# Self attention without its handover stalls, and the channel norm in three steps: one edit of a twelve-stage kernel

## The chip, the cores and the metric

The kernel runs on one core of a Trainium2 chip. The metric is the device time of one execution in microseconds (us). The engines are named as in the profile: PE is TensorE's matmuls, PEld its weight loads, DVE VectorE, ACT ScalarE, POOL GpSimd, SP the engine whose queue starts the transfers.

## The reference, cut to what matters

A tensor x of 16 blocks (batch) x 128 tokens x 256 channels passes through twelve sublayers, each `x = layernorm(x + sublayer(x))`. Three of them carry the change:

```python
# stage 1, self attention inside each block of 128 tokens
q, k, v = x @ Wq + bq, x @ Wk + bk, x @ Wv + bv
x = layernorm(x + softmax(q @ k.T / 16 + mask) @ v)
# stages 7 and 10, attention over channels (8 heads of 32 channels; the tokens are in pairs of halves)
ret = softmax(q.T @ k * scale) @ v.T           # q from x, k and v from a context of the same size
x = layernorm(x + ret)                         # stage 10 multiplies ret by gamma
# stage 11, int8-like feed forward; its weights are scaled by their largest magnitude
s = max(abs(W)); Wq = clip(round(W * 127 / s), -127, 127)
```

Stage 0, the gated delta rule, comes before stage 1 and only its end is touched.

## The kernel before, in words

The program is written engine by engine: each stage is a class with one method for each engine, and a stage's `order()` yields the steps that every engine walks in the same order. An engine executes its instructions strictly in that order and waits on counting semaphores (`wait_ge`). So a step that waits holds up all that is behind it on that engine. Tokens are worked on in 4 groups of 4 blocks (512 tokens). `X` holds x by tokens, `xT` its transposed copy. A sublayer ends for a group with a norm on DVE (4 `bn_stats` L211, 4 `bn_aggr` L214, a reciprocal root of 12 dependent operations on 4 numbers a partition L190 to L203, 4 scalings L227, which count `xn` up) and a "turn": 8 transposes on PE (L172), two copies on ACT (L181), which count `xt` up. `room[b]` is what must have happened before PSUM bank b may be written again.

**Delta rule, stage 0.** For the last group the steps are "close" (sum, L776), "stats", "scale" and "turn". At its end every bank is set to wait for the last turn: `for b in range(8): room[b] = c.xt.at(16)`.

**Self attention, stage 1.** The order is, for t = 0 to 4: "qk" (group t; 4 times 2 matmuls L285, 4 drains on ACT L896), "pt" (t - 1; 4 transposes L871, a copy L907), "v" (t; L291, 2 drains on DVE L920), "o" (t - 1; L880), "s" (t; scores L863, then on DVE scale and mask L924 and row maxima L927, then 4 exponentials on ACT L902), "close" (t - 1). "close" is on DVE the sum into the one tile R (L934) and the whole norm, and on PE and ACT the turn of the same group. ACT, DVE and SP enter the stage when the whole turn of stage 0 is done (`before`, `may_load`); PE waits for `dma[0] >= 64`, that is for all four transfers: weights, two biases and the mask, whose 1 MB comes in pieces of 512 bytes.

**Channel attention, stages 7 and 10** (Channels, ChannelsGamma). For t = 0 to 18 a step t works on block t and the two before it. PE runs "sh" (2 transposes of the negated maxima of block t - 1, L2498), "s" 0 (scores of block t, L2489), "t" 0 (transposed scores of block t - 1, L2510), "o" 0, "t" 1, "s" 1, "o" 1, "t" 2, "vt" (context of block t + 1 turned, L2478), "o" 2, "t" 3 (L2523 is "o"). DVE takes 4 maxima after each "s" (L2585, about 0.62 us each from start to start), shifts (L2591, "sh") and finishes block t - 3 (L2597 to L2605, "mul"). "t" 0 on PE waits for "sh" on DVE. POOL masks the operands of the next block (L2629, L2632) and v (L2638) when ACT has copied what "vt" turned. The norm of a group is "stats" (L211 to L203, all but the scalings) and "scale" (L227), at t = 6 and 7, 10 and 11, 14 and 15, and after the loop. Both stand between "t" 1 and "s" 1. The turn of the group is at t = 8, 12, 16 and at the end, after "vt", in bank 7 alone; stage 10 leaves its turns out.

**Beside stage 10** the steps of `Quant.BESIDE` prepare stage 11, one per t, behind "s" 1: "wmax" (the largest of each partition), "wall" (largest over the partitions: a transpose L2234, a maximum on DVE L2337, a broadcasting matmul L2236, four small DVE operations L2339 to L2342, all in bank 7), "wround" (ACT L2286, then POOL clips L2397), "wcast", and "xmax", "xround", "xclip", "xcast" for the first tokens. Within "wall" PE waits for DVE's maximum before it goes on to the matmul.

Of the kernel before, what the change touches and what calls it, by code (L numbers as in the profile page):

```python
# [65 lines left out]
class Core:  # L66
# [139 lines left out]
    def moments(self, dve, own, rows, st, sw, eps):  # L206

        for j, (row, ready) in enumerate(rows):
            if ready:
                dve.wait_ge(own.sem, ready)  # L210
            o = own(dve.bn_stats(st[:, j, 0:6], row))  # L211
        dve.wait_ge(own.sem, o)
        for j in range(4):
            o = own(dve.bn_aggr(st[:, j, 6:8], st[:, j, 0:6]))  # L214
        dve.wait_ge(own.sem, o)
        return self.rsqrt(dve, own, st[:, :, 7:8].rearrange("p a b -> p (a b)"), eps, [sw[:, blk(i, 4)] for i in range(3)])
# [78 lines left out]
class Delta(Stage):  # L295
# [131 lines left out]
    def order(self):  # L427


        for t in range(self.U + self.LAG + 5):  # L430
# [4 lines left out]
            for step, u in every:  # L435
                if 0 <= u < self.U and (step not in ("close", "stats", "scale", "turn") or u % 16 == 15):
                    yield step, u, u % self.RING, u // 16, u % 16

    def tensor(self, pe):
# [122 lines left out]
        for b in range(8):  # L562
            room[b] = c.xt.at(16)
# [248 lines left out]
class SelfAttention(Stage):  # L812


    def weights(self):
        c = self.c
        self.w, self.b, self.bv = c.f32("aw", 3, 2, D), c.f32("ab", 4), c.f32("abv", D)
        self.mask = c.f32("amask", NB, T)

    def load(self, sp):  # L820
        i = self.ins
        self.may_load(sp)
        self.fetch(sp, 0, (self.w[:, :, :, :], i["a_w"].rearrange("n (c p) f -> p n c f", p=128)), (self.b[:, :], i["a_b"]),
                   (self.bv[:, :], i["a_bv"]), (self.mask[:, :, :], i["mask_BxSxS2_ff0"].rearrange("b q k -> q b k")))

    def buffers(self):
        c = self.c
        self.QK, self.V = c.sets(2, "aQK", 2, 2, 512), c.sets(2, "aV", 4, D)
# [4 lines left out]
        self.vc, self.sm, self.mx = v("v", 8), v("s", 4), v("max", 4)  # L833

    def order(self):
        for t in range(5):
            for step, u in (("qk", t), ("pt", t - 1), ("v", t), ("o", t - 1), ("s", t), ("close", t - 1)):
                if 0 <= u < 4:
                    yield step, u, u % 2

    def tensor(self, pe):
        c, bank, room = self.c, self.c.bank, self.c.room
        pe.wait_ge(self.dma[0], 64)
        for step, g, s in self.order():
# [29 lines left out]
            elif step == "o":  # L874
                pe.wait_ge(*self.ptc.at(g + 1))
                pe.wait_ge(*self.vc.at(2 * g + 2))
                for b in range(4):
# [3 lines left out]
                    room[b // 2] = c.xn.at(4 * self.n + g + 1)  # L881
                t.then_inc(*self.o.up)
            elif step == "close":
                c.turn_tensor(pe, self.n, g, (2, 3))

    def scalar(self, act, own):
        c, bank = self.c, self.c.bank
        self.before(act)
        act.wait_ge(self.dma[0], 64)
        for step, g, s in self.order():  # L890
# [17 lines left out]
            elif step == "close":  # L908
                c.turn_scalar(act, self.n, g, (2, 3))

    def vector(self, dve, own):
        c, bank = self.c, self.c.bank
        self.before(dve)
        dve.wait_ge(self.dma[0], 64)
        for step, g, s in self.order():
# [6 lines left out]
            elif step == "s":  # L922
                dve.wait_ge(*self.sc.at(g + 1))
                dve.scalar_tensor_tensor(out=self.S[s][:, :, :], in0=g4(bank(6)), scalar=1.0 / 16, in1=self.mask[:, blk(g, 4), :],  # L924
# [6 lines left out]
            elif step == "close":  # L931
# [2468 lines left out]
```

## Time and profile before

| | |
|---|---|
| median of 3 runs | 4642.03 us (4641.69 to 4643.85) |
| profiled execution, its own time | 4642.03 us |
| its span, first to last instruction | 4640.2 us |
| mean granted TensorE clock | 0.901 of full |
| self attention with the norm and turn before it | 1178.4 to 1304.0 us of the span |
| channel attention, stages 7 and 10 | 2736.7 to 2976 us and 4274 to 4521 us |

The span is 1.8 us shorter than the execution's own time. A busy time is that of an engine's instructions; where an engine is idle the profile names the instruction of another engine whose signal ended the idle time.

### The profile page before, as it was taken

The page shows a single profiled execution, that of the slowest core. Times are in us where ns is not written, and L with a number is a line of the kernel's source. Part 1 is how long each engine was busy: PE and PEld are TensorE (multiplying, and loading weights), DVE is VectorE, ACT ScalarE, POOL GpSimd, SP SyncE. Part 2 cuts the span into 40 slices and gives each one's busy share as a digit, 9 for nine tenths or more (in the row PEclk, how much of TensorE's full clock was granted, in tenths as well). Part 3 has the DMA queues.
Part 4 walks back from the last instruction along what each step waited for, and adds up shares of the span by engine and source line. Part 5 has one row for each costly group of instructions (what it writes and reads, how often), then busy time and mean ns, then how long its engine had stood idle before and what let it go on. Part 6 is the DMA issues. An engine that isn't in the chain of part 4 may idle for free. (4 is left out here: it accounts for less than half of the span.)

```text
span 4640.2 us, 69825 instructions
## 1 busy us (share of the span) xinstructions
PE 3831.6 (83%) x25178; PEld 2327.9 (50%) x25196; DVE 3215.6 (69%) x7121; ACT 1966.2 (42%) x4633; POOL 1140.9 (25%) x1338
## 2 busy tenths in 40 slices
PE   7799999999615757778888889676999999897985
PEld 3466666656413435545455555453555555454543
DVE  7789989886376764432455557656888888886678
ACT  4466666655201013311333324324655556564345
POOL 2423333233021225220111122003332323233220
PEclk9899999999757878879899989888999999998797
DMA  2322222221101000020000000200000000001000
GB/s 63 75 61 65 62 65 63 56 56 42 39 31 31 1 0 21 1 67 0 20 1 1 1 28 2 113 1 0 1 1 1 1 1 1 1 1 44 1 1 19
DMA packets 220694, 120.64 MB, mean 26 GB/s; under 512 B 114881, under 2 KB 213057, under 8 KB 219137
## 3 DMA queue, kind: packets, MB, share of 16 engines
q1 hardware_dynamic: 220352, 116.17, 9.0%
q8 instruction: 204, 3.34, 0.3%
q14 instruction: 138, 1.12, 0.1%
HBM read 101.42 MB, written 14.68 MB: 25 GB/s over the span
## 5 line engine op out<-in xcount | busy, mean ns | idle before, releaser
L285 PE MATMUL ps<-xT,min 128*128 128x512 f32 (+1 forms) x1072 | 539.4, 633 | 7.7 <-DVE mZ L3121 5.4
L3126 DVE SCALAR_TENSOR_TENSOR macc<-ps,mcw,macc 128x508 f32<-128x508 f32 (+2 forms) x408 | 302.9, 743 | 149.7 <-ACT macc L3048 140.1
L3062 ACT ACTIVATE mE<-ps,mcol 128x128 f32<-128x128 f32 x1024 | 291.3, 370 | 8.1 <-PE ps L2960 1.0
L3212 POOL TENSOR_TENSOR mE<-mE,mCB 128x512 f32<-128x512 f32 x128 | 163.7, 1279 | 498.3 <-ACT mE L3062 498.3
L285 PEld LDWEIGHTS ps<-xT,min 128*128 128x128 f32 (+1 forms) x1072 | 184.9, 193 | 192.9 <-issue 182.6
L172 PE MATMUL ps<-ident,X 128*128 128x128 f32 x352 | 77.7, 388 | 239.9 <-DVE X L227 206.7
L2990 PE MATMUL ps<-mwo,macc 128*128 128x256 f32 x1024 | 245.4, 383 | 15.6 <-DVE macc L3160 15.6
L2553 ACT ACTIVATE hE<-ps 128x512 f32<-128x512 f32 x256 | 139.0, 595 | 248.9 <-PE ps L2510 248.9
L3219 POOL TENSOR_TENSOR mSQ<-mSQ,mtn 128x512 f32<-128x512 f32 x128 | 163.4, 1277 | 257.8 <-ACT mtn L3066 257.8
L2175 POOL TENSOR_TENSOR lP<-lP,lm 128x512 f32<-128x512 f32 x64 | 66.6, 1041 | 610.3 <-DVE lm L2157 610.3
L2990 PEld LDWEIGHTS ps<-mwo,macc 128*128 128x128 f32 x1024 | 185.8, 191 | 42.8 <-DVE macc L3160 21.2
L2091 ACT ACTIVATE lP<-ps,lm 128x128 f32<-128x128 f32 x256 | 90.6, 366 | 268.0 <-DVE lm L2153 268.0
L2585 DVE TENSOR_REDUCE hMX<-ps 128x2 f32<-128x512 f32 x256 | 159.0, 685 | 55.8 <-PE ps L2489 55.8
L181 ACT COPY xT<-ps 128x512 f32<-128x512 f32 x88 | 50.6, 587 | 342.5 <-PE ps L172 342.4
L803 POOL TENSOR_TENSOR dTB<-did,dNB 128x1024 f32<-128x1024 f32 (+1 forms) x10 | 29.2, 2919 | 665.9 <-DMA dNB<-d_N 601.3
L172 PEld LDWEIGHTS ps<-ident,X 128*128 128x128 f32 x352 | 60.5, 202 | 255.8 <-DVE X L227 214.8
L808 POOL TENSOR_TENSOR dTB<-dTB,dtmp 128x30 f32<-128x30 f32 (+11 forms) x300 | 170.1, 567 | 23.5
L709 DVE SCALAR_TENSOR_TENSOR dav<-ps,dsmall,dav 128x508 f32<-128x508 f32 (+2 forms) x192 | 142.4, 741 | 47.8 <-ACT dav L580 43.3
L709 DVE SCALAR_TENSOR_TENSOR daq<-ps,dsmall,daq 128x508 f32<-128x508 f32 (+2 forms) x192 | 142.5, 742 | 40.0 <-ACT daq L580 34.4
L2510 PE MATMUL ps<-hXE,hKE 32*128 32x256 f32 x1024 | 162.0, 438 | 8.1 <-ACT hE L2553 5.8
L807 POOL TENSOR_TENSOR dtmp<-dNB,dTB 128x30 f32<-128x30 f32 (+11 forms) x300 | 153.2, 511 | 23.5
L477 PE MATMUL ps<-dKQ 128*128 128x256 f32 x512 | 136.7, 394 | 26.7 <-ACT dO L655 19.0
(582 smaller groups left out, 9559.4 us busy)
## 6 DMA issues: line engine op xcount, KB each, us to landing
dwk<-in_L_attn_Wk SPq DMA_DIRECT2D x64, 128.0 KB, 2.3
dwq<-in_L_attn_Wq SPq DMA_DIRECT2D x64, 128.0 KB, 2.3
dwv<-in_L_attn_Wv SPq DMA_DIRECT2D x64, 128.0 KB, 2.4
dwg<-in_L_attn_Wg SPq DMA_DIRECT2D x64, 128.0 KB, 2.4
dwo<-in_L_attn_Wo SPq DMA_DIRECT2D x64, 128.0 KB, 2.6
min<-in_m_in SPq DMA_DIRECT2D x2, 4096.0 KB, 17.3
d_N<-dNT SPq DMA_DIRECT2D x256, 16.0 KB, 1.5
dTT<-d_TT SPq DMA_DIRECT2D x256, 16.0 KB, 1.9
```

Of the source, the lines that this page charges most:

```text
L285: t = pe.matmul(out, w[:, j, :], self.c.xT[:, j, blk(g, 512)], start=j == 0, stop=j == 1)
L709: x = dve.scalar_tensor_tensor(out=acc[:, :, 3 - j:T], in0=p[:, :, 0:T - 3 + j], scalar=small[:, 4 * k + j:4 * k + j + 1], in1=acc[:, :, 3 ...
L807: then(pool.tensor_tensor(part, bc(NB[:, s, s + 1:32], s, True), bc(TB[:, s, 0:s], 31 - s), ALU.mult))
L808: then(pool.tensor_tensor(low, low, part, ALU.subtract))
L2510: t = pe.matmul(bank(4 + i)[:, blk(lt, 256)], self.KE[x][r, e, blk(lt)], self.XE[x][r, e, :], start=True, stop=True)
L2553: a = act.activation(self.E[y][:, 2 * (2 * rr + i) + e, :, :], bank(4 + i).rearrange("p (n q) -> p n q", n=2), ACT.Exp, scale=0.25)
L2585: m = dve.tensor_reduce(self.MX[y][:, k, 32 * r:32 * r + 32:16], bank(r).rearrange("p (e n) -> p e n", e=2), AX.X, ALU.max, negate=True)
L2990: t = pe.matmul(bank(j // 2)[:, blk(j % 2, 256)], self.acc[s][:, blk(j)], self.wo[:, i, :], start=i == 0 and j % 2 == 0, stop=i == 31 and ...
L3062: x = act.activation(self.E[s][:, e, blk(j)], bank(4 + e)[:, blk(j)], ACT.Exp, bias=self.col[:, 4 * g + j, 0, 2 * i + e:2 * i + e + 1])
L3126: x = dve.scalar_tensor_tensor(out=acc[:, :, 3 - j:T], in0=p[:, :, 0:T - 3 + j], scalar=self.cw[:, i, j:j + 1], in1=acc[:, :, 3 - j:T], op ...
L3212: pool.tensor_tensor(g4(self.E[s][:, 0, :]), g4(self.E[s][:, 0, :]), self.CB[g % 2][:, :, :], ALU.mult).then_inc(*self.m0.up)
L3219: pool.tensor_tensor(self.SQ[g % 2][:, :], self.SQ[g % 2][:, :], self.tn[s][:, :], ALU.add).then_inc(*self.sqa.up)
```

## The change

Self attention: (1) its weights get a place that stage 0 does not use and are fetched without a wait; the mask is fetched apart, on a semaphore of its own, when stage 0's last norm is done, and only DVE's "s" step waits for it. (2) The turn of stage 0's last group moves out of stage 0 and behind the first "qk" and "v" ("last"). (3) "close" falls apart into "sum" (its own semaphore, two tiles R in turn), "norm" one round later, between "pt" and "v", and "turn" at the end of that round. Channel attention: the norm is in three steps, "stats", "rsqrt", "scale", at t = 6, 7, 8 and so on, all behind "s" 1 now; the turns are one t later. Beside stage 10 "wall" is in two steps, "wturn" and "wall", two t apart, and the later steps move.

```diff
@@ Delta
-                if 0 <= u < self.U and (step not in ("close", "stats", "scale", "turn") or u % 16 == 15):
+                if 0 <= u < self.U and (step not in ("close", "stats", "scale", "turn") or u % 16 == 15) and (step, u) != ("turn", self.U - 1):
...
-        for b in range(8):
-            room[b] = c.xt.at(16)
@@ SelfAttention
+    LOADS, PLACE, REST = 2, 154944, 0
...
     def load(self, sp):
         i = self.ins
-        self.may_load(sp)
         self.fetch(sp, 0, (self.w[:, :, :, :], i["a_w"].rearrange("n (c p) f -> p n c f", p=128)), (self.b[:, :], i["a_b"]),
-                   (self.bv[:, :], i["a_bv"]), (self.mask[:, :, :], i["mask_BxSxS2_ff0"].rearrange("b q k -> q b k")))
+                   (self.bv[:, :], i["a_bv"]))
+        sp.wait_ge(*self.c.xn.at(4 * self.n))
+        self.fetch(sp, 1, (self.mask[:, :, :], i["mask_BxSxS2_ff0"].rearrange("b q k -> q b k")))
...
+        self.mask, self.R = c.f32("amask", NB, T), [c.R, c.f32("aR", 4, D)]
...
     def order(self):
-        for t in range(5):
-            for step, u in (("qk", t), ("pt", t - 1), ("v", t), ("o", t - 1), ("s", t), ("close", t - 1)):
-                if 0 <= u < 4:
+
+        for t in range(6):
+            for step, u in (("qk", t), ("pt", t - 1), ("norm", t - 2), ("v", t), ("last", t), ("o", t - 1), ("sum", t - 1), ("s", t), ("turn", t - 2)):
+                if 0 <= u < (1 if step == "last" else 4):
                     yield step, u, u % 2
...
-        pe.wait_ge(self.dma[0], 64)
+        pe.wait_ge(self.dma[0], 48)
...
-                    room[b // 2] = c.xn.at(4 * self.n + g + 1)
+                    room[b // 2] = self.su.at(g + 1)
                 t.then_inc(*self.o.up)
-            elif step == "close":
+            elif step == "last":
+                c.turn_tensor(pe, self.n - 1, 3, (2, 3))
+            elif step == "turn":
                 c.turn_tensor(pe, self.n, g, (2, 3))
...
     def scalar(self, act, own):
         c, bank = self.c, self.c.bank
-        self.before(act)
-        act.wait_ge(self.dma[0], 64)
+        act.wait_ge(*c.xn.at(4 * self.n))
+        act.wait_ge(self.dma[0], 48)
...
     def vector(self, dve, own):
         c, bank = self.c, self.c.bank
-        self.before(dve)
-        dve.wait_ge(self.dma[0], 64)
+        dve.wait_ge(self.dma[0], 48)
...
                 dve.wait_ge(*self.sc.at(g + 1))
+                dve.wait_ge(self.dma[1], 16)
...
-            elif step == "close":
+            elif step == "sum":
                 dve.wait_ge(*self.o.at(g + 1))
                 dve.wait_ge(own.sem, self.r)
-                sums = [own(dve.scalar_tensor_tensor(out=c.R[:, j, :], in0=bank(j // 2)[:, blk(j % 2, 256)], scalar=m[:, 8 + j:9 + j],
-                                                     in1=c.X[:, 4 * g + j, :], op0=ALU.mult, op1=ALU.add)) for j in range(4)]
-                c.norm_vector(dve, own, self.n, g, sums)
+                for j in range(4):
+                    x = dve.scalar_tensor_tensor(out=self.R[s][:, j, :], in0=bank(j // 2)[:, blk(j % 2, 256)], scalar=m[:, 8 + j:9 + j],
+                                                 in1=c.X[:, 4 * g + j, :], op0=ALU.mult, op1=ALU.add)
+                x.then_inc(*self.su.up)
+            elif step == "norm":
+                dve.wait_ge(*self.su.at(g + 1))
+                c.norm_vector(dve, own, self.n, g, [0] * 4, self.R[s])
@@ Quant
-    BESIDE = {3: ("wmax", 0), 4: ("wmax", 1), 5: ("wall", 0), 6: ("wall", 1), 7: ("wround", 0), 8: ("wround", 1), 10: ("wcast", 0), 12: ("wcast", 1),
-              13: ("xmax", 0), 14: ("xround", 0), 15: ("xclip", 0), 16: ("xcast", 0)}
+    BESIDE = {3: ("wmax", 0), 4: ("wmax", 1), 5: ("wturn", 0), 6: ("wturn", 1), 7: ("wall", 0), 8: ("wall", 1), 9: ("wround", 0), 10: ("wround", 1),
+              11: ("wcast", 0), 12: ("wcast", 1), 13: ("xmax", 0), 14: ("xround", 0), 15: ("xclip", 0), 16: ("xcast", 0)}
...
     def tensor_step(self, pe, step, u):
         c, bank, room = self.c, self.c.bank, self.c.room
-        if step == "wall":
+        if step == "wturn":
             pe.wait_ge(*room[7])
             pe.wait_ge(*self.wm.at(u + 1))
             pe.transpose(bank(7)[0:1, 0:128], self.g1[:, u:u + 1], c.ident[:, :]).then_inc(*self.wt.up)
+            room[7] = self.wm.at(u + 3)
+        elif step == "wall":
+            pe.wait_ge(*room[7])
@@ Channels
-                if step == "t" and k == 1:
-                    for n, first in (("stats", 6), ("scale", 7)):
+                if step == "s" and k == 1:
+                    for n, first in (("stats", 6), ("rsqrt", 7), ("scale", 8)):
                         if t >= first and (t - first) % 4 == 0:
                             yield n, (t - first) // 4, 0
-                if step == "s" and k == 1 and t in self.ASIDE:
-                    yield "aside", *self.ASIDE[t]
-                if step == "vt" and t >= 8 and t % 4 == 0 and self.TURNS:
-                    yield "turn", (t - 8) // 4, 0
+                    if t in self.ASIDE:
+                        yield "aside", *self.ASIDE[t]
+                if step == "vt" and t >= 9 and t % 4 == 1 and self.TURNS:
+                    yield "turn", (t - 9) // 4, 0
+        yield "rsqrt", 3, 0
```

`moments` is cut in two helpers, `moments_of` (L211, L214) and `rsqrt_of` (L190 to L203), which issue the same instructions.

## Rows read from the trace of the kernel before

**Rows 1.** The page: busy time of each engine, share of the span, instructions.

```profile
PE 3831.6 (83%) x25178; PEld 2327.9 (50%) x25196; DVE 3215.6 (69%) x7121; ACT 1966.2 (42%) x4633; POOL 1140.9 (25%) x1338
```

**Rows 2.** Stretch of self attention: busy us of each engine (instructions), clock, DMA.

```profile
1178.36:1304.04 125.68, 73.98 (x280) 50.00 (x280) 44.47 (x160) 25.24 (x62) 0.00 (x0) 0.79 0.10 35
```

**Rows 3.** What PE waited for there: us in total, times, longest.

```profile
PE ps L172 <- DVE X L227: 40.2, 5, 8.6
PE ps L285 <- DMA amask<-in_mask_BxSxS_ff: 10.2, 1, 10.2
```

**Rows 4.** Timeline, stage 0's end and the start: start, us, instruction, [idle before].

```profile
1178.36 1.42 DVE L776 TENSOR_TENSOR R<-ps,X 128x256 f32<-128x256 f32 x4 [3.87 <-PE ps L555]
...
1184.05 1.38 DVE L227 TENSOR_SCALAR X<-R,st,rsq 128x256 f32<-128x256 f32 x4
...
1189.77 0.84 SPq L276 DMA_DIRECT2D amask<-in_mask_BxSxS_ff  x1
...
1197.63 9.70 PE L285 MATMUL ps<-xT,aw 128*128 128x512 f32 x16 [10.17 <-DMA amask<-in_mask_BxSxS_ff]
```

**Rows 5.** Timeline, the second round of PE: first qk, pt, and the scores.

```profile
1212.40 7.03 PE L285 MATMUL ps<-xT,aw 128*128 128x512 f32 x16
1219.27 0.60 PE L871 MATMUL ps<-ident,aP 128*128 128x128 f32 x4
...
1224.89 1.95 PE L863 MATMUL ps<-aQK 128*128 128x128 f32 x16
```

**Rows 6.** Timeline: the third sum, PE's stall behind it, the stage's last copy.

```profile
1281.41 1.65 DVE L934 SCALAR_TENSOR_TENSOR R<-ps,am,X 128x256 f32<-128x256 f32 x4
...
1288.64 1.97 PE L172 MATMUL ps<-ident,X 128*128 128x128 f32 x8 [8.60 <-DVE X L227]
...
1303.42 0.59 ACT L181 COPY xT<-ps 128x512 f32<-128x512 f32 x1 [0.27 <-PE ps L172]
```

**Rows 7.** Stage 7: one plain step t; then t = 6 and 7; 10 and 11; 14 and 15.

```profile
2798.32:2809.08 10.76, 10.76 (x136) 6.45 (x137) 8.27 (x14) 5.20 (x11) 3.41 (x7) 1.00 0.01 3
2809.08:2837.84 28.76, 24.72 (x268) 14.70 (x269) 23.09 (x51) 10.39 (x21) 6.83 (x13) 0.88 0.00 1
2863.80:2892.48 28.68, 24.67 (x268) 14.41 (x268) 23.08 (x50) 10.39 (x21) 6.82 (x13) 0.88 0.01 2
2918.44:2946.57 28.13, 24.31 (x262) 13.94 (x262) 22.58 (x50) 10.06 (x20) 3.54 (x7) 0.88 0.01 1
```

**Rows 8.** Timeline around the "stats" of t = 6 in stage 7.

```profile
2817.13 0.17 DVE L190 TENSOR_SCALAR rsq<-st 128x4 f32<-128x4 f32 x1
...
2818.55 1.43 POOL L2638 TENSOR_TENSOR hVE<-hV,hrp 128x256 f32<-128x256 f32 x2 [7.35 <-PE ps L2523]
...
2820.48 0.42 DVE L203 SCALAR_TENSOR_TENSOR rsq<-rsq 128x4 f32<-128x4 f32 x1
...
2823.44 0.41 PE L2498 MATMUL ps<-ident,hMX 128*128 128x128 f32 x2 [4.01 <-DVE hMX L2585]
```

**Rows 9.** Timelines of POOL and DVE at the end of a plain step.

```profile
2807.79 1.42 POOL L2638 TENSOR_TENSOR hVE<-hV,hrp 128x256 f32<-128x256 f32 x2 [7.35 <-PE ps L2523]
...
2809.08 0.88 DVE L2591 SCALAR_TENSOR_TENSOR hXE<-ps,hpar,hXE 128x256 f32<-128x256 f32 x2 [2.19 <-PE ps L2498]
```

**Rows 10.** Stage 10: the twelve steps t = 4 to 15; then t = 5, 6 and 8.

```profile
4329.56:4504.15 174.59, 154.44 (x1588) 90.05 (x1588) 125.86 (x245) 71.26 (x128) 43.66 (x70) 0.82 0.01 1
...
4340.32:4358.23 17.91, 15.10 (x139) 8.26 (x139) 9.04 (x20) 5.45 (x12) 4.07 (x9) 0.77 0.00 1
4358.23:4381.88 23.65, 19.73 (x139) 10.79 (x139) 12.80 (x39) 5.20 (x11) 2.88 (x5) 0.57 0.01 1
4395.19:4410.69 15.50, 13.93 (x132) 8.20 (x132) 8.41 (x14) 7.07 (x12) 5.28 (x8) 0.78 0.00 1
```

**Rows 11.** Timeline, PE at two short waits in stage 10.

```profile
4349.18 0.38 PE L2236 MATMUL ps<-qg,ones 1*128 1x1 f32 x2 [2.81 <-DVE qg L2337]
...
4396.73 1.20 PE L2489 MATMUL ps<-hKE,hXE 32*128 32x256 f32 x16 [1.57 <-issue]
```

More of the change, by code:

```diff
@@ L204, in rsqrt, with moments_of @@
         return o
-    def moments(self, dve, own, rows, st, sw, eps):
+    def moments_of(self, dve, own, rows, st):
         for j, (row, ready) in enumerate(rows):
@@ L214, in moments, with rsqrt_of @@
             o = own(dve.bn_aggr(st[:, j, 6:8], st[:, j, 0:6]))
+        return o
+    def rsqrt_of(self, dve, own, st, sw, eps):
+        return self.rsqrt(dve, own, st[:, :, 7:8].rearrange("p a b -> p (a b)"), eps, [sw[:, blk(i, 4)] for i in range(3)])
+    def moments(self, dve, own, rows, st, sw, eps):
+        o = self.moments_of(dve, own, rows, st)
         dve.wait_ge(own.sem, o)
-        return self.rsqrt(dve, own, st[:, :, 7:8].rearrange("p a b -> p (a b)"), eps, [sw[:, blk(i, 4)] for i in range(3)])
+        return self.rsqrt_of(dve, own, st, sw, eps)
     def norm_vector(self, dve, own, n, g, sums, R=None):
@@ L832, in buffers @@
         self.qkc, self.ex, self.ptc = s("qk", 16), s("exp", 4), s("pt", 4)
[L833 removed]
+        self.vc, self.sm, self.mx, self.su = v("v", 8), v("s", 4), v("max", 4), v("sum", 4)
     def order(self):
[L836 to L838 removed]
+        for t in range(6):
+            for step, u in (("qk", t), ("pt", t - 1), ("norm", t - 2), ("v", t), ("last", t), ("o", t - 1), ("sum", t - 1), ("s", t), ("turn", t - 2)):
+                if 0 <= u < (1 if step == "last" else 4):
                     yield step, u, u % 2
@@ L907, in scalar @@
                 act.copy(self.PT[s][:, :], bank(7)).then_inc(*self.ptc.up)
-            elif step == "close":
+            elif step == "last":
+                c.turn_scalar(act, self.n - 1, 3, (2, 3))
+            elif step == "turn":
                 c.turn_scalar(act, self.n, g, (2, 3))
@@ L2334, in vector_step @@
             dve.tensor_reduce(g1[:, u:u + 1], self.flat[u], AX.X, ALU.max, apply_absolute_value=True).then_inc(*self.wm.up)
-        elif step == "wall":
+        elif step == "wturn":
             dve.wait_ge(*self.wt.at(u + 1))
             dve.tensor_reduce(g1[0:1, 2 + u:3 + u], bank(7)[0:1, 0:128], AX.X, ALU.max).then_inc(*self.wm.up)
+        elif step == "wall":
             dve.wait_ge(*self.wb.at(u + 1))
@@ L2607, in vector @@
                 dve.wait_ge(*self.sum.at(4 * b + 4))
-                last = c.moments(dve, own, [(self.R[b % 2][:, i, :], 0) for i in range(4)], c.st, c.rsq, 1e-5)
+                last = c.moments_of(dve, own, [(self.R[b % 2][:, i, :], 0) for i in range(4)], c.st)
+            elif step == "rsqrt":
+                dve.wait_ge(own.sem, last)
+                last = c.rsqrt_of(dve, own, c.st, c.rsq, 1e-5)
             elif step == "scale":
```

2 lines of the change are left out of this document (removed).

## The prediction

> **What bounds the kernel now.** I read the page first. PE is busy 83% of the span and DVE 69% [rows 1], so neither share says what a stage is worth, and each changed stage has to be read by itself. Then the stretch of self attention by windows: from the last product of stage 0 to the last copy of stage 1 it is 125.7 us long, PE works 74 of them and DVE 44 [rows 2]. No engine is full, so waits set the length. The waits of that stretch name them: PE stood 40.2 us, five times and at most 8.6 us, for the scaled X of a norm, and once 10.2 us for the mask [rows 3]. The timeline shows the pattern: DVE sums a group, norms it, and only then does PE turn it and go on to the next group's products, which don't need that norm at all [rows 6]. For the channel stages I took windows from one "sh" of DVE to the next, since one such period is one step t. A plain step is 10.76 us with PE busy 10.76: PE is full, at the full clock. The two steps that hold a norm's "stats" and "scale" take 28.76, 28.68 and 28.13 us, 21.0 us more in all than six plain ones [rows 7]. In stage 10 the twelve steps t = 4 to 15 take 174.6 us [rows 10], 45.5 more than twelve plain ones.
>
> **The sum goes against the profiled execution's own time, 4642.0 us, which is also the median of the runs shown;** 1.8 us of it lie outside the span and stay.
>
> **Self attention, the start.** The first products begin at 1197.6 because PE asks for all four transfers and the mask lands last, 7.8 us after its issue at 1189.8; the issue itself waits for stage 0's turn [rows 4]. After the change the weights are fetched while stage 0 still runs, and the bank resets are gone, so PE waits only for banks 0 and 1, which the sum at 1178.36 frees 1.42 us later: 1179.8 [rows 4]. That is 17.8 us earlier. The norm of stage 0 (until 1184.05 + 1.38 = 1185.4, that is 5.65 us) then lies beside the first products, ACT's first drain starts at 1185.4 instead of when PE would allow it, and PE does not notice, since "v" uses other banks. The moved turn costs PE 1.0 us of the full clock between "v" and "s" (8 transposes, 1.97 us at half clock [rows 6]). The mask is issued at 1185.4 and lands by 1193.3 if it takes its 7.8 us again; DVE needs it when the first scores are done, 14.8 us behind 1179.8 as now behind 1197.6 (until 1212.40) plus the turn: 1195.6. So the mask is hidden with 2 us to spare. If it were not, DVE alone would wait; behind it stand the maxima and exponentials of group 0, while PE has the 6.9 us of the second "qk" to do. The next stage's fetches stand behind the mask on SP and start when the moved turn is copied, 1194.6 instead of 1190.6, and are wanted some 60 us later.
>
> **The rounds.** A round of PE at the full clock is 14.3 us: from 1212.40 to 1224.89 and another 1.8 for the scores [rows 5]. Each now carries a turn, but two rounds behind its sum, when the norm is long done: 15.3 us. DVE's work in a round is a norm (5.6), the sum (1.65), and 3.0 for drains, scores and maxima, 10.3 of 15.3: it does not become the bound. ACT has 6.3. Starting from 1195.6 the scores end at 1209.9 (no turn in that round), 1225.2 and 1240.5. There "qk" runs at 6.87 us each time instead of 8.61 and 9.08 behind a stall, for PE no longer idles long enough to come back at half clock.
>
> **The end.** Behind the last scores DVE does mask and maxima (1.45), the norm of group 2 (5.6; meanwhile PE and ACT finish group 3's products), the sum (1.65) and the norm (5.6) of group 3, then a turn and its copies (2.65): 17.0 us, so the stage ends at 1257.5. It ended at 1303.42 + 0.59 = 1304.0 [rows 6]: **46.5 us gained.** Bounds: if the first products find the full clock, they take 6.87 instead of 9.70 [rows 4, 5], 2.8 more gained, unless the mask then binds; if each of three rounds loses a microsecond in handovers, 3 less. So 43 to 49.5.
>
> **Channel attention, stage 7.** What does the 21.0 us consist of? In t = 6 the norm's first part delays the second maxima, PE idles 4.01 us [rows 8] and comes back at half clock, which fills t = 7 (clock 0.88 over both [rows 7]). The new slot is behind the second maxima, where DVE idles 2.19 us before "sh" in every plain step [rows 9]. "stats" (1.41 + 0.38 and gaps, 1.85) and "scale" (1.4) fit: cost 0. The root does not quite: alone its 12 operations take 2.4 us, 0.2 more than the slot. But the slot opens at 2809.08 - 2.19 = 2806.9 and POOL's work begins at 2807.8, 0.9 us into it [rows 9]. The timeline shows what POOL does to the root: from 2817.13 to 2820.90 it takes 3.8 us though 8 of its 12 operations start ahead of POOL, and one that takes 0.16 to 0.17 alone takes 0.42 beside it [rows 8]. In the new slot only 4 start ahead; six more end one by one with POOL's six instructions of a step, 3.4 us together [rows 7], and two follow: 0.9 + 3.4 + 0.3 = 4.6, that is 2.4 over the slot. The Trainium skill (SBUF — State Buffer, "Who interferes with whom") speaks against this placing: a DVE operation with two SBUF inputs and a GpSimd one that reads SBUF exclude each other for the whole instruction. By the rule all of the root behind POOL's start goes at POOL's pace, the 2.4; read without it, the cost would be 0.2; the trace's 0.42 agrees with it.
>
> So "sh" is late by 2.4 in one step of each group and PE idles as long. Will it come back at half clock? After 2.81 us idle and even after 1.57 us it did [rows 11]; the second of these made its step 15.50 us, 4.74 over [rows 10]. A restart costs up to 3.2 us (what t = 7 has over a plain step). I take 2.0 for it, 4.4 for each group against 7.0 now: 3 x 2.6 = **8 us gained**. Bounds: 3 x (7.0 - 5.6) = 4 and 3 x (7.0 - 0.2) = 20. The turns move by a step and keep their price (t = 8 has it now): 0. The last group's tail is unchanged.
>
> **Stage 10.** The 45.5 us over are, by step: t = 5 ("wall") 7.15, t = 6 ("stats", "wall") 12.9, t = 8 4.74 [rows 10], the other nine together 20.7. Of 7.15, 2.81 is PE waiting in the middle of "wall" [rows 11], the rest the half clock behind it. After the change:
> - t = 5, "wturn": the maximum on DVE follows the second maxima (0.3), and bank 7 is wanted by "vt" only 2.1 us behind the transpose: 1.1.
> - t = 6 to 8: the small operations now stand behind "stats", root and scale on DVE, while bank 7 is held: "vt" waits about 2.6, 3.7 and 2.6 us, which is as long as the 2.81 that cost 7.15. I take 17.5 for the three. Between 9.5 (waits alone) and 21 (three times 7.15).
> - "wround" twice: POOL's clip makes the next operands late, as it does now (the 1.57 and 4.74): 6.2, same price two steps later.
> - the root at t = 11: 4.4 as in stage 7; t = 15: 1.5, for POOL has no block to prepare there; "stats" at t = 10 and 14 and "scale" at 12: 0.
>
> That is 30.7 against 45.5: **15 us gained**, between 8 and 27.
>
> **Sum:** 46.5 + 8 + 15 = 69.5; 4642.0 - 69.5 = **4572.5 us**.
>
> **Rivals.**
> - *The channel stages give nothing.* The root beside POOL is slow, each short idle restarts PE at half clock, and bank 7 held behind the norm eats what the split of "wall" frees. For it: 1.57 us of idling was enough [rows 11]. Against: the longest idles, 4.0 in t = 6 and the doubled one of stage 10, do go. Time: 4642.0 - 46.5 = 4595.5. It decides when the root costs 7 a group and t = 6 to 8 cost 27.
> - *The slots hold all.* POOL misses the root, PE keeps its clock: 20 + 27 + 49 gained, 4546. Against: the 0.42 beside POOL.
> - *Self attention finds another chain.* A round could be closed by sum, mask, maxima, exponentials and transposes through DVE and ACT, or norms could hold up V's drains, so that only the start and half of the three stalls is won: 17.8 + 13 = 31 instead of 46.5, with the rest 54: 4588. Against: DVE has 5 us free in a round.
> - *Slower, through the SP queue.* The mask is fetched late and the whole softmax waits for it. It would have to land 69.5 us behind the 1195.6 to turn the sign; it takes 7.8 [rows 4], and nothing stands before it. At 80 us it would give 4652.
>
> **How the numbers follow.** Chances: forecast, with its own range 4560 to 4584, 0.58; channel stages near nothing 0.15; slots hold all 0.10; another chain in self attention 0.15; slower or no change by the queue or something alike 0.02. A measurement of this kernel can tell about 0.2%, 9 us, from no change. All cases but the last give more than 9 us: faster 0.98, same 0.01, slower 0.01. The range leaves out half of "hold all" and a part of the two weaker cases: 4550 to 4596.
>
> **What would show it.** In the profile after: PE's first L285 of self attention near 1180, no wait of PE for L227 over 3 us until the last turn, and the stage's last copy near 1257.5. In stage 7 the pairs t = 6, 7 at 26 us instead of 28.7, with the root at 4 to 5 us beside POOL. In stage 10 t = 5 under 12 us, t = 6 to 8 at 16 us each, t = 14 plain. Wrong it would be by the clock: if PE does not fall to half clock behind idles of 2 to 3 us, both channel stages gain twice as much.

## The result and the profile after

| | before | after |
|---|---|---|
| median | 4642.03 us | 4574.57 us (3 runs, 4571.93 to 4582.10) |
| ratio | | 0.9857, 95% interval 0.9835 to 0.9880 |
| span of the profiled execution | 4640.2 | 4572.8 |
| mean granted clock | 0.901 | 0.906 |

67.5 us less (by the interval 56 to 77), where 69.5 were forecast (4572.5). The same comparison made again (experiment 10) gave 60.0 less, so the agreement to 2 us is closer than the measurement can vouch for. The page's line of busy time (answers to [rows 1]) says as little of the change as before:

```profile
PE 3819.8 (84%) x25196; PEld 2320.8 (51%) x25196; DVE 3208.8 (70%) x7121; ACT 1962.1 (43%) x4633; POOL 1140.9 (25%) x1338
```

So I cut both traces at the same landmarks and compared the pieces. The landmarks are DVE's last sum of stage 0, the last copy of self attention, and the "sh" of DVE in the channel stages (hXE written from PSUM). Positive is time saved:

```
piece                                    before    after    saved   forecast
to the last sum of stage 0              1178.36  1175.41     3.0      0
self attention, to its last copy         125.68    77.63    48.0     46.5
then to stage 7's "sh" of t = 1         1446.5   1446.6     -0.1      0
stage 7, "sh" of t = 1 to 16             196.05   188.36     7.7      8
its tail, to the next stage's first op    29.32    31.04    -1.7      0
stages 8 and 9, to "sh" of t = 1        1316.5   1316.0      0.5      0
stage 10, "sh" of t = 1 to 4              37.15    39.95    -2.8      0
stage 10, t = 4 to 15                    174.59   159.73    14.9     15
the rest                                 136.05   138.09    -2.0      0
sum                                     4640.2   4572.8     67.4     69.5
```

**Self attention.** The window answers to [rows 2] (it runs on for 1.2 us behind the stage's last copy), the waits to [rows 3] (columns as there):

```profile
1175.41:1254.20 78.79, 66.36 (x280) 46.38 (x280) 45.98 (x161) 24.03 (x62) 0.00 (x0) 0.91 0.13 45
```

```profile
PE ps L172 <- DVE X L235: 5.9, 1, 5.9
PE ps L882 <- ACT aP L915: 2.4, 1, 2.4
PE ps L293 <- DVE R L782: 1.6, 1, 1.6
PE ps L891 <- ACT aPT L920: 0.7, 1, 0.7
```

Before, these waits were 51.1 us, the 50.4 of [rows 3] and 0.7 at "o"; 10.6 are left. PE's work shrank from 74.0 to 66.4 us with as many instructions, since the granted clock rose from 0.79 to 0.91. The timeline answers to [rows 4 to 6]; L293 is "qk", L882 "pt", L891 "o", L874 the scores, L172 a turn:

```profile
1176.98 7.11 PE L293 MATMUL ps<-xT,aw 128*128 128x512 f32 x16 [1.60 <-DVE R L782]
...
1190.03 7.03 PE L293 MATMUL ps<-xT,aw 128*128 128x512 f32 x16
...
1204.53 7.10 PE L293 MATMUL ps<-xT,aw 128*128 128x512 f32 x16
...
1219.75 7.03 PE L293 MATMUL ps<-xT,aw 128*128 128x512 f32 x16
...
1237.46 1.09 PE L882 MATMUL ps<-ident,aP 128*128 128x128 f32 x4 [2.40 <-ACT aP L915]
1239.22 3.78 PE L891 MATMUL ps<-aV,aPT 128*128 128x256 f32 x8 [0.68 <-ACT aPT L920]
```

The first products start 1.57 us behind the sum's start (1.42 forecast; 19.27 before, from 1178.36 to 1197.63) and take 7.11 us, the full clock. Then two rounds lead to the fourth "qk" without a wait, 14.5 and 15.2 us, the second with a turn in it. The weights had been issued at 1121.31. The mask was issued on SP's queue at 1182.57 and landed 6.6 us later, at 1189.2. DVE's first use of it came at 1190.23, and what DVE had waited for was PE's scores:

```profile
1190.23 0.69 DVE L939 SCALAR_TENSOR_TENSOR aS<-ps,amask 128x512 f32<-128x512 f32 x1 [1.97 <-PE ps L874]
```

So the mask was hidden, with 1.0 us to spare where 2 were forecast.

**Stage 7.** Windows, columns as in [rows 7]: t = 6, 7, 8 and the turn's step 9 of the first group:

```profile
2758.26:2769.02 10.76, 10.76 (x136) 6.44 (x136) 9.95 (x21) 5.20 (x11) 3.39 (x7) 1.00 0.01 2
2769.02:2781.84 12.82, 11.79 (x148) 7.05 (x148) 12.14 (x26) 5.92 (x12) 5.46 (x11) 1.00 0.00 1
2781.84:2794.21 12.37, 11.46 (x120) 6.28 (x120) 9.53 (x18) 4.47 (x9) 1.35 (x3) 0.86 0.01 1
2794.21:2810.72 16.51, 14.66 (x144) 8.34 (x144) 8.26 (x13) 6.61 (x14) 4.11 (x9) 0.80 0.00 1
```

"stats" (t = 6) costs nothing. The root (t = 7) makes "sh" 2.06 us late. The timelines of DVE and POOL there answer to [rows 8, 9]:

```profile
2778.50 0.74 DVE L203 SCALAR_TENSOR_TENSOR rsq<-rsq 128x4 f32<-128x4 f32 x1
2779.27 0.65 DVE L199 SCALAR_TENSOR_TENSOR rsq<-rsq 128x4 f32<-128x4 f32 x1
...
2780.85 0.17 DVE L199 SCALAR_TENSOR_TENSOR rsq<-rsq 128x4 f32<-128x4 f32 x1
2781.05 0.33 DVE L201 TENSOR_TENSOR rsq<-rsq 128x4 f32<-128x4 f32 x1
2781.41 0.50 DVE L203 SCALAR_TENSOR_TENSOR rsq<-rsq 128x4 f32<-128x4 f32 x1
```

```profile
2778.49 1.41 POOL L2667 TENSOR_TENSOR hVE<-hV,hrp 128x256 f32<-128x256 f32 x2 [7.37 <-PE ps L2549]
2779.88 0.93 POOL L2658 TENSOR_SCALAR hXE<-X,hpar 128x256 f32<-128x256 f32 x2
2780.79 1.11 POOL L2661 TENSOR_SCALAR hKE<-hctx,hpar,hrow 128x256 f32<-128x256 f32 x2
```

The root begins at 2777.50. Its five operations ahead of POOL's start at 2778.49 take 0.16 to 0.17 us each. Of the seven beside POOL six take 0.33 to 0.74 us, and one, at 2780.85, took 0.17 there too.

**Stage 10.** Windows, t = 4 to 15, then t = 5 to 8 (answers to [rows 10]), and PE's waits at "vt" in t = 6 to 8 (answers to [rows 11]):

```profile
4274.98:4434.71 159.73, 144.58 (x1588) 85.03 (x1588) 120.91 (x241) 72.33 (x129) 43.57 (x70) 0.89 0.01 2
4285.73:4297.51 11.78, 11.03 (x137) 6.53 (x137) 8.52 (x15) 5.30 (x11) 3.40 (x7) 1.00 0.00 1
4297.51:4312.23 14.72, 12.27 (x137) 7.11 (x137) 10.18 (x23) 5.55 (x12) 3.97 (x9) 0.90 0.01 2
4312.23:4332.11 19.88, 16.49 (x138) 8.98 (x138) 10.73 (x29) 5.29 (x11) 3.47 (x8) 0.67 0.00 1
4332.11:4350.58 18.47, 16.14 (x138) 9.00 (x138) 10.14 (x21) 5.30 (x11) 2.87 (x5) 0.68 0.00 1
```

```profile
4308.08 0.44 PE L2504 MATMUL ps<-ident,hctx 128*128 128x128 f32 x2 [2.45 <-DVE qg L2361]
...
4326.92 0.66 PE L2504 MATMUL ps<-ident,hctx 128*128 128x128 f32 x2 [3.39 <-DVE qg L2367]
...
4346.04 0.44 PE L2504 MATMUL ps<-ident,hctx 128*128 128x128 f32 x2 [2.33 <-DVE qg L2367]
```

### The profile page after: what moved, and what is told of

The parts are those of the page before. It is cut to its first block and busy times, and to the rows that moved or that the text cites. A ratio compares the mean times of both kernels' runs of the same rounds, so it can differ in the third digit from the quotient of the medians.

```text
span 4572.8 us, 69849 instructions
## 1 busy us (share of the span) xinstructions
PE 3819.8 (84%) x25196; PEld 2320.8 (51%) x25196; DVE 3208.8 (70%) x7121; ACT 1962.1 (43%) x4633; POOL 1140.9 (25%) x1338
## 5 line engine op out<-in xcount | busy, mean ns | idle before, releaser
L293 PE MATMUL ps<-xT,min 128*128 128x512 f32 (+1 forms) x1072 | 538.2, 631 | 7.3 <-DVE mZ L3150 5.0
L293 PEld LDWEIGHTS ps<-xT,min 128*128 128x128 f32 (+1 forms) x1072 | 184.1, 192 | 191.7 <-issue 181.8
L3019 PE MATMUL ps<-mwo,macc 128*128 128x256 f32 x1024 | 245.3, 383 | 15.6 <-DVE macc L3189 15.6
L172 PE MATMUL ps<-ident,X 128*128 128x128 f32 x352 | 74.6, 377 | 205.2 <-DVE X L235 172.3
L2536 PE MATMUL ps<-hXE,hKE 32*128 32x256 f32 x1024 | 164.3, 443 | 13.9 <-DVE hXE L2617 8.1
L172 PEld LDWEIGHTS ps<-ident,X 128*128 128x128 f32 x352 | 58.6, 195 | 220.3 <-DVE X L235 178.9
L485 PE MATMUL ps<-dKQ 128*128 128x256 f32 x512 | 138.5, 398 | 26.4 <-ACT dO L661 17.5
```

Of the source, the lines that this page charges most:

```text
L293: t = pe.matmul(out, w[:, j, :], self.c.xT[:, j, blk(g, 512)], start=j == 0, stop=j == 1)
L2536: t = pe.matmul(bank(4 + i)[:, blk(lt, 256)], self.KE[x][r, e, blk(lt)], self.XE[x][r, e, :], start=True, stop=True)
L3019: t = pe.matmul(bank(j // 2)[:, blk(j % 2, 256)], self.acc[s][:, blk(j)], self.wo[:, i, :], start=i == 0 and j % 2 == 0, stop=i == 31 and ...
```

## The experiments

The kernel before was run again beside each batch; its medians were 4640.6 (experiments 1 to 4), 4646.0 (5 to 8) and 4637.5 us (9, 10). Pieces are those of the table above, from each kernel's one profiled execution; experiment 10 shows how far they vary in one and the same program.

**1 and 2. One half of the change each.** The first takes the hunks of Delta and SelfAttention alone, the second those of Channels and Quant alone.

> All of the change in self attention, none of it in the channel stages. My theory (the self attention gain is the stage's own and nothing is given back later): the stretch from the last sum of stage 0 to the last copy of stage 1 takes 77.6 us as in the whole change (125.7 before), and the kernel is 48 us faster than before, 4594. Rival (part of it came from elsewhere or is given back in later stages): the stretch is 77.6 but the total differs from 4594 by more than 6 us.

Measured: 4593.12 us, ratio 0.9894 (0.9879 to 0.9909). Self attention took 75.9 us; stage 7's steps 196.0 and its tail 29.3, as before.

> All of the change in the channel stages and the weight scaling beside stage 10, none in self attention. My theory: the sixteen steps of stage 7 take 188 us instead of 196, those of stage 10 about 200 instead of 212, and the total falls by 15 to 20 us, to 4622 to 4627. Rival (the channel parts only shift idle time and restarts of PE's clock about): under 9 us, no measurable change.

Measured: 4630.98 us, ratio 0.9974 (0.9962 to 0.9985), 9.6 us less (7 to 18 by the interval) and less than I expected. The profiled execution, 4617.44 us, was the fastest of the seven, so its pieces add up to more than the median shows: 14.1 us gained in stage 7's steps, 9.9 in stage 10's t = 4 to 15, and 6.9 between self attention and stage 7, where nothing was changed. Stage 7's tail took 34.35 instead of 29.32, and 2.6 us were lost behind t = 16 of stage 10. I had not counted these two places. The two medians together (47.5 + 9.6 = 57) are 10 us under the 67.5 of the whole change, but 3 us under the 60.0 that experiment 10 measured for it, so this is no evidence of a joint effect.

**3 and 4. Self attention, its start and its rounds apart.** The third keeps the early fetch and the moved turn, with sum and norm back in one round; the fourth splits the rounds and keeps the start of before (one order shown for each):

```diff
 # 3
-("qk", t), ("pt", t - 1), ("norm", t - 2), ("v", t), ("last", t), ("o", t - 1), ("sum", t - 1), ("s", t), ("turn", t - 2)
+("qk", t), ("pt", t - 1), ("v", t), ("last", t), ("o", t - 1), ("s", t), ("sum", t - 1), ("norm", t - 1), ("turn", t - 1)
 # 4
-("qk", t), ("pt", t - 1), ("norm", t - 2), ("v", t), ("last", t), ("o", t - 1), ("sum", t - 1), ("s", t), ("turn", t - 2)
+("qk", t), ("pt", t - 1), ("norm", t - 2), ("v", t), ("o", t - 1), ("sum", t - 1), ("s", t), ("turn", t - 2)
```

> Self attention with its early weights, the mask apart and the first products ahead of the last turn, but sum, norm and turn of a group in one piece as before. My theory (start and rounds are separate gains): the start gives 17.8 us for the earlier first product, plus up to 2.8 for the full clock, minus 1 for the turn; the three stalls of 8.6 us and the restarts at half clock stay: the stretch takes 105 to 109 us, and the kernel is 17 to 20 us faster. Rival (the mask or ACT's first drains hold the first group back once the rest is early): the stretch takes over 112.

Measured: 4626.85 us, ratio 0.9958 (0.9944 to 0.9971); the stretch took 107.6 us, 18.1 less. The median is 13.7 us less, where I expected 17 to 20, but the stretch is in its range of 105 to 109. PE still waited for the norms, four times now:

```profile
PE ps L172 <- DVE X L235: 33.6, 4, 8.7
```

> Self attention with sum, norm and turn in separate steps, but entered as before: last turn in stage 0, weights and mask fetched behind it, PE waits for both. My theory: PE stands still for no norm until the last turn, three stalls of 8.6 us and two restarts at half clock (about 4 us) go, the order of the end gains 1 to 2 less: the stretch takes 96 to 100 us, 27 us faster. Rival (the rounds gain only because the first group is early): over 104.

Measured: 4613.20 us, ratio 0.9937 (0.9920 to 0.9953); the stretch took 96.5 us, 29.2 less. What it keeps is the mask's wait and two norms:

```profile
PE ps L172 <- DVE X L235: 12.9, 2, 7.2
PE ps L293 <- DMA amask<-in_mask_BxSxS_ff: 10.5, 1, 10.5
```

18.1 + 29.2 = 47.3, and the whole gave 48.0: the two parts of self attention add up, and each of the forecast's two sources is seen by itself. (In this stretch profiles of the same self attention differ by up to 1.7 us.)

**5. The norm in three steps, "wall" left whole.** Only the hunks of Channels; `BESIDE` stays as before.

> Only the norm of the channel stages in three steps behind the second maxima; the weight scaling stays in one step (wall at t = 5 and 6), self attention as before. My theory: stage 7's sixteen steps take 188 us as in the whole change. In stage 10 wall 0 at t = 5 costs its 7 us again and wall 1 at t = 6 about as much (it stands behind stats on DVE), but t = 7 and 8 no longer hold a wall, so the steps t = 4 to 15 take 160 to 168. Rival (the split of wall is what gains in stage 10, the norm's does nothing there): 172 or more.

Measured: one run of 4637.48 us. Stage 7's steps took 188.61, the same as after. Stage 10's t = 4 to 15 took 164.81, and experiment 2, which has the split of "wall" as well, took 164.68. In this pair the split by itself gave nothing: it took 13.9 us out of t = 5 and 6 (18.46 and 23.01 to 11.78 and 15.78), and t = 7 to 11, where the second half of "wall" and "wround" now are, took 13.8 more. With the split, though, the changed kernel took 159.73 in one profile and 165.34 in the other. What these runs show of the split is between nothing and 5 us.

**6. The step beside stage 10 ahead of the norm's.** One exchange in `Channels.order`; "vt" then should not wait for the root while bank 7 is held:

```diff
                 if step == "s" and k == 1:
+                    if t in self.ASIDE:
+                        yield "aside", *self.ASIDE[t]
                     for n, first in (("stats", 6), ("rsqrt", 7), ("scale", 8)):
...
-                    if t in self.ASIDE:
-                        yield "aside", *self.ASIDE[t]
```

> The whole change, but in each step of stage 10 the weight scaling's operation goes ahead of the norm's on every engine. My theory (in t = 6, 7, 8 PE waits for bank 7, which is held until DVE's small operations behind stats, root and scale are done): t = 6, 7, 8 took 14.7, 19.9 and 18.5 us in the changed kernel and take 12, 15 and 13 now, 13 us less, the total 4562. Rival (the clock's restarts make these steps long whatever holds bank 7, or the root pushed back by 0.8 us costs what is freed): under 4 us less.

Measured: 4571.14 us, ratio 0.9837 (0.9816 to 0.9858). Windows of t = 4 to 15, then t = 6 to 8:

```profile
4281.75:4429.34 147.59, 137.27 (x1588) 80.96 (x1588) 121.68 (x242) 72.33 (x129) 43.55 (x70) 0.94 0.01 2
4304.27:4316.05 11.78, 11.03 (x137) 6.53 (x138) 10.21 (x23) 5.31 (x11) 3.11 (x7) 1.00 0.01 3
4316.05:4328.27 12.22, 10.85 (x138) 6.52 (x142) 11.47 (x29) 5.36 (x11) 3.73 (x7) 1.00 0.01 1
4328.27:4341.75 13.48, 12.25 (x138) 6.98 (x138) 10.05 (x23) 5.49 (x12) 3.45 (x7) 0.88 0.00 1
```

t = 6 to 8 took 37.5 us instead of 53.1, the value of both profiles of the changed kernel. The waits of "vt" fell from 2.45, 3.39 and 2.33 to 0.75, 1.37 and 1.23 us, and the clock stayed at 1.00 in two of the three steps. The whole was 74.9 us under the kernel before beside it, where the changed kernel was 67.5 and 60.0 under it in its two comparisons: 7 to 15 us gained, where I expected 13. Stage 7's tail, which this edit does not touch, took 37.8 us here, as in the changed kernel's second profile and not as in its first (31.0).

**7. The root in two halves.** The first turn of its iteration at t = 7, the other two at t = 8, "scale" at 9, the turns a step later (10, 14, 18), so that no piece reaches far into POOL's work:

```diff
-                    for n, first in (("stats", 6), ("rsqrt", 7), ("scale", 8)):
+                    for n, first in (("stats", 6), ("rsqrt", 7), ("rsqrt2", 8), ("scale", 9)):
...
-                if step == "vt" and t >= 9 and t % 4 == 1 and self.TURNS:
-                    yield "turn", (t - 9) // 4, 0
+                if step == "vt" and t >= 10 and t % 4 == 2 and self.TURNS:
+                    yield "turn", (t - 10) // 4, 0
```

> The whole change, but the root is cut into two steps of 6 operations, so that stats, root, root, scale are at t = 6, 7, 8, 9 and the turn at t = 10. My theory (the root overruns the slot of 2.2 us because POOL slows it, sh is late by 2 us and PE's clock falls behind the idle time): each half ends inside the slot or 0.3 us behind it; in stage 7 the steps t = 7 and 8 (12.8 and 12.4 us) fall to about 10.9, t = 11 likewise, 4 to 6 us less over the sixteen steps. Rival (the excess is the clock's and comes from the turn and from other idle time): the sixteen steps stay within 2 us of 188.

Measured: 4563.06 us, ratio 0.9820 (0.9796 to 0.9844). Stage 7's steps took 178.27 us, with t = 7, 8 and 9 plain: 10.1 less, where I expected 4 to 6. The last operation of the first half and POOL's first start together:

```profile
2778.65 0.16 DVE L214 SCALAR_TENSOR_TENSOR rsq<-rsq 128x4 f32<-128x4 f32 x1
```

```profile
2778.64 1.44 POOL L2690 TENSOR_TENSOR hVE<-hV,hrp 128x256 f32<-128x256 f32 x2 [7.37 <-PE ps L2570]
```

**8. POOL's work made small.** The masking of v for blocks 8 and 12 covers 4 of 128 columns, and that of x and context for blocks 9 and 13 covers 8 of 256; the rest of it is left out. Root and order are those of after.

> The whole change, but POOL works on 8 or 4 columns instead of 256 or 128 for the operands that it prepares beside the first two roots (blocks 8, 9, 12, 13); this leaves out most of that masking. My theory: the root at t = 7 of stage 7, 4.4 us beside POOL, takes 2.4 to 3.0, and the step 10.8 to 11.3 us instead of 12.8; PE does not idle, so t = 8 is a plain 10.8 instead of 12.4. Rival (the twelve dependent operations are slow in that place for another reason): root over 3.8 and t = 7 still over 12.

Measured: one run of 4572.25 us. The root took 2.39 us from first to last (2778.65 to 2781.04) instead of 4.41, t = 7 and 8 were 10.78 and 10.75, and stage 7's steps took 178.30 us, to 0.03 the time that the halves gave. Two edits that share nothing but keeping root and POOL's long work apart give the same stage: POOL beside the root is the cause of these 10 us.

**9 and 10. Both edits together, and the changed kernel once more beside it.** Experiment 9 has the edits of 6 and 7; experiment 10 is the changed kernel, unaltered.

> The changed kernel with both edits that helped, the step beside stage 10 ahead of the norm's steps and the root in two halves (1 + 2 turns of the iteration, at t = 7, 8; scale at t = 9, turns a step later). If the two causes are separate, POOL's instructions gating a root that does not fit, and bank 7 held behind the norm's operations, the gains add: stage 7's sixteen steps as with the halves alone, 178.3 us or somewhat less, and stage 10's t = 4 to 15 near 147.6 less the 3.7 that the root cost at t = 11, 144. The whole: 4572.8 - 10 - 16 = 4547 of span if stage 7's tail keeps TensorE's full clock (29 us), 4556 if it falls to half clock there (38 us). Rival: both edits took away the same idle time, the root standing between the aside step and its bank; then stage 10 stays at 147 to 148 and the whole at 4560 to 4563, no better than the halves alone.

Measured: **4546.96 us** (5 runs, 4541.34 to 4552.11), ratio 0.9808 (0.9793 to 0.9822). Stage 7's steps 178.26, its tail 28.97, stage 10's t = 4 to 15 148.0 (147.6 in experiment 6, 160.2 in 7). So in stage 10 the halves add nothing to the exchange, 148 where I expected 144, as its rival had it; but the whole is far under the rival's 4560, since stage 7 and its tail keep what the halves gave (some 7 us of the span of 4539.5 are by chance, the stretch of 1439.6 us between self attention and stage 7, see the last section).

> The changed kernel unaltered, beside the other on the same chip, for a second look at the pieces that varied between executions. If the tail of stage 7 (from the last sh to the next stage's first statistics) depends on which steps of the kernel leave TensorE idle, it is 31.0 us again, as in the first profile; if it is chance, it may be 38. Total: 4565 to 4577, ratio 0.984 to 0.987.

Measured: 4577.51 us (4573.54 to 4580.30), ratio 0.9870 (0.9856 to 0.9884). The tail took 37.82 us this time, where the first profile had 31.04. The expectation's other case holds: it is one program with two values. The tail is not the only such piece:

```
the changed kernel, in us                first    second profile
self attention to stage 7                1446.6   1440.1
stage 7, "sh" of t = 1 to 16              188.36   188.61
its tail                                   31.04    37.82
stage 10, "sh" of t = 1 to 4               39.95    37.09
stage 10, t = 4 to 15                     159.73   165.34
```

The last line differs in t = 9 to 12 alone, 51.2 and 56.8 us, at a granted clock of 0.94 and 0.83. Experiments 2 and 5 are another pair: ahead of stage 10 their instructions are the same, and stage 7's steps took 181.96 and 188.61. Experiment 9 ran 30.6 us faster than the changed kernel on the same chip.

## Why the prediction was right, and where its steps were not

**Self attention, 46.5 forecast, 48.0 measured.** The start was right in cause and place: the first products came 17.7 us earlier against 17.8, and experiment 3, which has the start alone, gained 18.1. The upper bound's condition came true, for the first "qk" ran at the full clock, 7.11 instead of the 9.70 that [rows 4] show: 2.6 more. The rounds, forecast at 14.3 without and 15.3 with a turn, took 14.5 and 15.2. Of the three the prediction gave two a turn ahead of the last scores; by the order of the steps only one has it, which is 1.0 more. From the end of the scores (1234.0) to the end of the stage it took 19.0 us against 17.0, for group 3's products did not end beside group 2's norm, as forecast: "pt" waited 2.4 us for ACT's exponentials, "o" behind it ran at half clock, 3.78 us where the rounds have 1.89, and DVE waited 1.8 us for "o" before the last sum. 2.6 and 1.0 more and 2.0 less make the 1.5 us but for 0.1. The last norm and turn closed the stage as said. The rival that sees another chain close the rounds is refuted: from the first "qk" to the last scores no wait of PE is on the list. So is the one through SP's queue: DVE did not wait for the mask.

**Stage 7's steps, 8 forecast, 7.7 measured, and two terms off that cancel.** The second profile gave 7.4, experiment 2 14.1. Over plain steps, in us:

```
                          before              after                  forecast after
norm, first group       4.05 + 3.19     2.06 + 1.61 = 3.7            4.4
norm, second            4.05 + 3.11     1.54 + 3.26 = 4.8            4.4
norm, third             3.54 + 3.07     0                            4.4
turn, first             4.45            5.75 + 3.27 = 9.0            4.45
turn, second            4.44            4.71                         4.45
```

The root beside POOL was right in mechanism and near in size (2.06 late against 2.4); experiment 8 shows it. Five operations started ahead of POOL instead of four, six were slowed, as many as forecast, and one behind them was not. At t = 15 I charged 4.4 although POOL has no block to prepare there, which I did count in stage 10: it cost nothing. *The step that failed in size is "the turns move by a step and keep their price".* The first turn's own waits are as before (1.17 and 0.68 us), but TensorE came back to the full clock later behind them. The turn's step is the last window shown for stage 7 above; this is the window of the step behind it, and then those of both steps before the change:

```profile
2810.72:2824.75 14.03, 14.03 (x136) 8.08 (x137) 10.05 (x22) 4.95 (x10) 2.75 (x5) 0.75 0.01 2
```

```profile
2837.84:2853.05 15.21, 13.36 (x144) 7.76 (x145) 8.26 (x14) 6.36 (x13) 3.40 (x7) 0.89 0.00 1
2853.05:2863.80 10.75, 10.75 (x136) 6.43 (x136) 8.27 (x13) 5.19 (x11) 3.40 (x7) 1.00 0.01 2
```

In the second step after the change PE is busy all of its 14.03 us at a clock of 0.75: nothing waits, it is only slow. It was the same in experiments 7 and 8 (16.77 and 13.75, 16.41 and 14.14), where the root costs nothing, so it is not the root's doing. Nor is it that of the turn's new place, for in experiment 2 the same turn at the same t, with the same two waits, kept its price to 0.03 us:

```profile
2836.28:2851.52 15.24, 13.39 (x144) 7.79 (x145) 8.27 (x14) 6.36 (x13) 3.48 (x7) 0.89 0.00 1
2851.52:2862.27 10.75, 10.75 (x136) 6.45 (x136) 9.95 (x21) 5.19 (x11) 3.36 (x7) 1.00 0.01 3
```

Experiment 5, with the same instructions up to there, took 16.52 and 14.01. So the forecast of 4.45 is one of two values and the changed kernel twice had the other, 9.0; what decides between them was not settled. 4.5 of the 6.65 us between experiments 2 and 5 in stage 7 lie in these two steps.

**"The last group's tail is unchanged" failed too.** It took 29.32 us in all four profiles of the old channel steps, and 31.04, 34.35 and four times 37.8 with the new ones and the turns at t = 9, 13, 17. The instructions of the first products behind the last "sh", before and then after:

```profile
2947.50 1.13 PE L2510 MATMUL ps<-hXE,hKE 32*128 32x256 f32 x8 [0.97 <-DVE hXE L2591]
2948.56 1.93 PE L2523 MATMUL ps<-hE,hVE 128*32 128x256 f32 x32
...
2953.90 0.66 PE L172 MATMUL ps<-ident,X 128*128 128x128 f32 x4
...
2956.21 1.07 PE L2523 MATMUL ps<-hE,hone 128*32 128x256 f32 x16
```

```profile
2888.96 1.69 PE L2536 MATMUL ps<-hXE,hKE 32*128 32x256 f32 x8 [0.97 <-DVE hXE L2617]
2890.58 3.01 PE L2549 MATMUL ps<-hE,hVE 128*32 128x256 f32 x32
...
2903.45 0.66 PE L172 MATMUL ps<-ident,X 128*128 128x128 f32 x4
...
2905.37 1.07 PE L2549 MATMUL ps<-hE,hone 128*32 128x256 f32 x16
```

Behind the same wait of 0.97 us the first two groups of products took 1.13 and 1.93 us before, 1.69 and 3.01 after: 1.6 us more by the clock, nearly all of the 1.7. The third group's turn is not the reason. At t = 17 it stands ahead of block 15's last product and holds it up by 1.9 us, but at t = 16 it had stood in this tail as well, ahead of the same product, and taken 2.3. In experiment 10 the half clock lasted longer behind the same wait, which makes the 37.82:

```profile
2884.88 1.96 PE L2536 MATMUL ps<-hXE,hKE 32*128 32x256 f32 x8 [0.97 <-DVE hXE L2617]
2886.77 3.64 PE L2549 MATMUL ps<-hE,hVE 128*32 128x256 f32 x32
```

Why this wait never brought the half clock with the old steps and always did with the new ones was not settled. The halves put the turn at t = 18, behind block 15's last product: that takes some 2 us off, and the tail is 28.97 in experiments 7 and 9, with the clock as in the first profile of after (2.84 and 2.86 us in place of the 3.01).

**Stage 10, 15 forecast, 14.9 and 9.3 measured in t = 4 to 15.** The prediction's terms against the first profile: t = 5 cost 1.0 (1.1 forecast). The waits at bank 7 were 2.45, 3.39 and 2.33 against 2.6, 3.7 and 2.6; the three steps cost 20.8 over plain against 17.5, since the half clock lasted through t = 7 and 8. "wround" took 4.5 against 6.2, the root at t = 11 3.7 against 4.4, t = 15 0.65 against 1.5. So the sum of 30.7 came out by terms that cancel, and by luck of the profile: in the second, "wround" took 5.9 and the root with the step behind it 7.9, and the gain was 9.3. The mis-sized term is t = 6 to 8, 20.8 in both profiles, near the prediction's own bound of 21; the sign that it named, 16 us each, did not come (14.7, 19.9, 18.5). The prediction named bank 7 held behind the norm as the cost that eats the split, and experiment 6 shows it: the exchange alone takes 15.6 us out of these three steps. The 2.8 us more at t = 1 to 4 were no effect of the change: t = 1 took 14.37 in the first profile of after and 11.91 in the second, and both values occur with the old channel steps too (14.37 in experiments 1 and 4, 11.92 before and in experiment 3). The bounds of 8 and 27 stand without their working; the range given for t = 6 to 8 alone makes 11 to 23.

**The rivals.** "The channel stages give nothing" came near in experiment 2 (9.6 us) and in the second profile of after (5.6), but not by its conditions: the root cost 3.7, 4.8 and 0 where it wanted 7 a group, t = 6 to 8 cost 20.8 where it wanted 27, and most of what was missing lay in steps at a lower clock: at the turn, in the tail and, in the second profile, at t = 9 to 12 of stage 10. "The slots hold all" is what experiment 9 approaches with two more edits.

**The total came out 2 us off by cancellation and luck.** Of the channel stages 23 us were forecast. With the tail, t = 1 to 4 and the rest they gave 16 in the first profile and 5.6 in the second, so this half was forecast 7 to 17 us too high. Self attention was 1.5 too low, and 3 of the 67 came from stage 0's end, which lay between 1174.3 and 1178.9 in all kernels whatever was changed.

## What to carry to other kernels

Small dependent operations put into an idle slot cost by what else runs in the slot: look whether GpSimd starts inside it, and cut the chain so that each piece ends by then. When a step is split so that its wait goes, write down the order of the pieces behind one another too: a bank held by a tiny step that stood behind a longer one gave back most or all of what the split had won, and exchanging two lines took 15.6 us out of three steps. Look at what stands ahead of the product that closes a stage: the third group's turn stood there before and after the change, and moving it behind took some 2 us off the tail. And before an agreement to a few microseconds is taken for a proof of the terms, profile the same program twice.

## What the runs showed of the hardware

- Four-element DVE operations, 0.16 to 0.17 us alone, took 0.33 to 0.74 us beside POOL's masking, and twelve of them 4.41 instead of 2.39 us. This fits the rule of the Trainium skill (SBUF — State Buffer, "Who interferes with whom") by which a DVE operation with two SBUF inputs and GpSimd's reads shut each other out: the slowed ones all have two. It is no test of it, for the operations with one input ran before POOL began, and some with two ran at 0.16 to 0.17 us while POOL was busy (2780.85 in after, 2778.65 in experiment 7).
- One and the same program took two times in several places, and the granted clock differs with them. Stage 7's tail was 31.04 and 37.82 us in the changed kernel, t = 9 to 12 of stage 10 51.2 and 56.8 us at a clock of 0.94 and 0.83, and stage 7's steps were 181.96 and 188.61 us in experiments 2 and 5. The stretch from self attention to stage 7 was 1446.6 and 1440.1 us; these 6.5 us arise in one place, between 873 and 1087 us behind self attention's last copy, where PE comes back to the full clock sooner. The windows from 955 to 980 us behind that copy, in the first profile of after and then in the second:

```profile
2208.04:2233.04 25.00, 24.38 (x114) 13.54 (x113) 10.82 (x20) 9.59 (x39) 3.12 (x3) 0.89 0.00 1
```

```profile
2210.27:2235.27 25.00, 23.77 (x125) 13.28 (x124) 14.06 (x26) 9.85 (x38) 4.16 (x4) 1.00 0.00 1
```

So a difference of 7 us between two single profiles of this kernel says nothing by itself; the pieces have to be compared, and whole kernels only by several runs of each.
